# Gated cross-attention on one core: half of the next batch's context tiles turned a step earlier, and other instruction orders on all engines

## The reference

```python
q = (query @ wq)   # 32 heads of 128, rotated by position
k = (key @ wk)     # 8 groups of 128, each shared by 4 heads, rotated by position
v = (value @ wv)   # 8 groups of 128
raw = einsum('bhqd,bhkd->bhqk', q, k) / sqrt(128)
attn = softmax(raw + mask, axis=-1)
out = einsum('bhqk,bhkd->bhqd', attn, v) @ wo

x = x + tanh(g_xattn) * cross_attention(layernorm(x), ctx, ctx, mask)
x = x + tanh(g_ffn) * lora_experts(layernorm(x))
```

## Time and profile before

| | us |
|---|---|
| median of three runs (1941.01 to 1945.7) | 1941.62 |
| the profiled execution | 1944.6 |
| its span, first to last instruction | 1942.7 |

### The profile page before, as it was taken

The page is one execution under the profiler, slowest core; times in us unless marked ns, Lnnn a source line. Parts: engine busy times, 40 slices in busy tenths (PEclk is TensorE's granted clock), DMA queues, the critical chain, the costliest instruction groups (busy, mean ns, idle before and its releaser), DMA issues. The chain is left out here.

```text
span 1942.7 us, 36348 instructions
## 1 busy us (share of the span) xinstructions
PE 1863.1 (96%) x12454; PEld 1706.5 (88%) x12454; DVE 1552.9 (80%) x2598; ACT 1019.1 (52%) x1882; POOL 1194.0 (61%) x990
## 2 busy tenths in 40 slices
PE   7989999999999999999999999999999999999688
PEld 7979998999889998999899988999899988999576
DVE  6768888888878888888888888888788888888244
ACT  5645555555555555555655555555455555556232
POOL 5627666666666674777566666776576656777300
PEclk9999999999999999999999999999999999999788
DMA  6622111112111111221112211111121110211270
GB/s 221 251 73 37 36 21 32 26 37 31 31 32 34 32 16 33 37 36 21 31 26 36 31 23 30 32 35 20 31 32 31 30 33 13 56 16 21 60 249 20
DMA packets 75303, 91.98 MB, mean 47 GB/s; under 512 B 22948, under 2 KB 49828, under 8 KB 75144
## 3 DMA queue, kind: packets, MB, share of 16 engines
q1 hardware_dynamic: 74136, 83.44, 20.2%
q10 hardware_dynamic: 1008, 6.42, 0.8%
HBM read 74.07 MB, written 15.77 MB: 46 GB/s over the span
## 5 line engine op out<-in xcount | busy, mean ns | idle before, releaser
L699 POOL TENSOR_TENSOR pT<-prob,pT 125x448 fp32r<-125x448 f32 x384 | 483.8, 1271 | 86.1 <-ACT pT L824 86.1
L881 PE MATMUL low_banks<-wv_hi,cT_hi 128*125 128x256 f32 x1536 | 434.4, 283 | 0.0
L881 PE MATMUL low_banks<-wv_hi,cT_lo 128*125 128x256 f32 x1536 | 432.7, 282 | 0.0
L881 PE MATMUL low_banks<-wv_lo,cT_hi 128*125 128x256 f32 x1536 | 432.3, 281 | 0.0
L765 ACT ACTIVATE k_work<-low_banks 64x500 f32<-64x500 f32 x384 | 223.8, 583 | 193.3 <-PE low_banks L865 186.1
L1081 DVE TENSOR_TENSOR prob<-t_banks,mask_t 125x448 f32<-125x448 f32 x384 | 235.3, 618 | 110.2 <-PE t_banks L916 95.4
L693 POOL TENSOR_TENSOR k_lo<-k_work,k_hi 128x500 fp32r<-128x500 f32 x192 | 253.8, 1322 | 110.1 <-ACT k_hi L773 110.1
L865 PE MATMUL low_banks<-cT_hi,wk_hi 128*128 128x500 f32 x768 | 315.5, 411 | 0.4 <-DVE cT_lo L1052 0.4
L710 POOL TENSOR_TENSOR sums<-sums,prob 125x448 f32<-125x448 f32 x252 | 291.0, 1155 | 26.8 <-ACT prob L818 25.8
L865 PE MATMUL low_banks<-cT_lo,wk_hi 128*128 128x500 f32 x768 | 298.8, 389 | 0.0
L865 PE MATMUL low_banks<-cT_hi,wk_lo 128*128 128x500 f32 x768 | 298.5, 389 | 0.0
(11 more groups left out here) (152 smaller groups left out, 3857.0 us busy)
## 6 DMA issues: line engine op xcount, KB each, us to landing
stage<-in_ctx_dram SPq DMA_DIRECT2D x72, 250.0 KB
inv_b<-inv_by_head SPq DMA_DIRECT2D x65, 112.0 KB, 4.8
attn_by_head<-attn SPq DMA_DIRECT2D x65, 112.0 KB, 1.7
wq_raw<-in_L_xattn_wq_dram SPq DMA_DIRECT2D x7, 1024.0 KB, 6.8
q_raw<-q_by_head SPq DMA_DIRECT2D x64, 112.0 KB, 4.9
head_rows<-in_ctx_dram SPq DMA_DIRECT2D x24, 250.0 KB
stage<-in_L_xattn_wo_dram SPq DMA_DIRECT2D x4, 1024.0 KB, 6.9
k_work<-in_L_xattn_wo_dram SPq DMA_DIRECT2D x4, 1024.0 KB, 7.7
```

Source lines behind the costliest of these rows:

```text
L699: nc.gpsimd.tensor_tensor(pT[:, j % PT_SLOTS, :, 1, :], pair(j), f32(pT[:, j % PT_SLOTS, :, 0, :]), ALU.subtract).then_inc(p_lo, 1)
L881: mm = nc.tensor.matmul(v_banks[0:ST, m % 2, t * PAIR:(t + 1) * PAIR], cT[a][:, d, tile * ST:(tile + 1) * ST], w[1][mv][:, d, g * DH:g * D ...
```

## The change

Six of the twelve context tiles (C0 to C5) are turned in the step before the turn, which gets a row "ahead" of its own; C6 to C11 stay in the turn, where the mask turnings W0 and W1 move from the front to the middle. ScalarE copies the first pair of masked scores into the running maximum's bank ("copy", begin_top), so that DVE's first maximum reads it there rather than from SBUF. The rows of all kinds of step are written in another order. In the last step the projection of the first two groups goes by pass over all heads (O0h, O1h, O2h, then R0, R1, R2 for the second group), so that the high by high pass waits for no low part; later groups are projected by pass too. The first quarter of POOL's low part of wo moves into the step before, ahead of its last work. The third and fourth groups' loads are issued within the last batch's last step, the third's ahead of store_attn; the last inverse's round trip and the third group's low parts move behind the barrier.

```diff
-    "turn": ("W0 W1 C0 X C1 M C2 C3 V00 Y C4 K00 C5 K01 C6 K02 K03 C7 C8 PV0 V01 K10 K11 K12 C9 K13 V10 C10 C11 "
-           "V11 PV1 S0 S1 K20 K21 K22 K23 S2 PV2 S3 V20 V21 PV3 PV4 S4 S5 PV5"),
...
+    "ahead": ("K00 K01 K02 K03 V30 K10 K11 X C0 C1 M K12 K13 K20 K21 V31 Y PV0 K22 C2 C3 V40 S0 K23 V41 S1 V50 PV1 "
+            "PV2 S2 S3 V51 C4 C5 PV3 PV4 PV5 S4 S5"),
+    "turn": ("K00 K01 C6 C7 V00 K02 C8 X K03 M C9 Y V01 K10 K11 K12 C10 C11 K13 V10 PV0 W0 W1 K20 K21 K22 K23 V11 "
+           "PV1 PV2 V20 S0 S1 V21 S2 S3 PV3 S4 PV4 S5 PV5"),
...
-    "last": "X O00 M O01 Y O02 O03 PV0 PV1 PV2 PV3 PV4 PV5 Y1 O1",
...
+    "last": "O00 O01 O02 X O03 M O10 O11 Y O12 O13 O20 O21 O22 O23 R0 PV0 PV1 PV2 R1 R2 PV3 PV4 PV5 Y1",
...
+def context_item(b, m):
+
+    g = HKV - 2 if ("C", m) in t_fills(PE_STEP, "ahead") else HKV - 1
+    return t_item(b, g, "C", m, False)
...
-def output_loads(sp, shared, wo, attn_dram, i, passed):
-    for u in range(2):
-
-        sp.wait_ge(shared.attn_lo, i * 2 + (u + 1))
-        wait_apart(sp, shared.wo_lo, i * 2 + (u + 1), passed)
-        load_wo(sp, shared, wo, i * 2 + (2 + u), u)
-        load_attn(sp, shared, attn_dram, i * 2 + (2 + u), u)
+def output_load(sp, shared, wo, attn_dram, n, passed):
+
+    sp.wait_ge(shared.attn_lo, n - 1)
+    wait_apart(sp, shared.wo_lo, n - 1, passed)
+    load_wo(sp, shared, wo, n, n % 2)
+    load_attn(sp, shared, attn_dram, n, n % 2)
 
...
-                        wait_apart(sp, t_ready, t_item(b, g, "C", m - STAGE_RING, False) + 1, sp_passed)
+                        wait_apart(sp, t_ready, context_item(b, m - STAGE_RING) + 1, sp_passed)
                         load_context(nc, sp, shared, ctx_v, b + 1, m)
...
-                store_attn(b, g)
+                if g == HKV - 1 and last:
+                    output_load(sp, shared, wo, attn_dram, 2, sp_passed)
+                store_attn(sp, shared, attn_dram, b, g)
...
-        spread_inverse(B, 0)
-        output_loads(sp, shared, wo, attn_dram, 0, sp_passed)
-        store_attn(B, 0)
+        output_load(sp, shared, wo, attn_dram, 3, sp_passed)
...
-                    for h in range(REP):
-                        wo_low_head(h)
+                    wo_low_head(n)
...
+        def begin_top(n, item):
+
+            act.wait_ge(t_free, item + (RING + 1))
+            if n > 0:
+
+                act.wait_ge(subbed, n * PT)
+            nc.scalar.activation(run_max, pair(0), ACT.Copy).then_inc(top_begun, 1)
...
+                if what == "copy":
+                    begin_top(b * HKV + g + 1, t_item(b, g, "S", 0, last))
...
+                if what in ("O", "R"):
+                    u, part = ("O", "R").index(what), n[0]
+                    if what == "O" and n == (0, 0):
 
                         pe.wait_ge(k_rotated, k_item(b, g, NC - 1) + 1)
                         pe.wait_ge(v_free, v_item(b, g - 1, V_AHEAD - 1) + (RING + 1))
-                        pe.wait_ge(shared.wo_lo, 1)
-                    if h < REP - 1:
-                        pe.wait_ge(pieces, REP - 1 + h + 1)
-                    else:
-                        pe.wait_ge(shared.attn_lo, 1)
-                    mm = project_head(nc, shared, h, 0, True)
-                    if h == REP - 1:
+                    if part == 0:
+                        pe.wait_ge(shared.wo_hi, u + 1)
+                        pe.wait_ge(shared.attn_hi, u + 1)
+                    if part == 1:
+                        pe.wait_ge(*((pieces, n[1] + 1) if what == "O" and n[1] < REP - 1 else (shared.wo_lo, u + 1)))
+                    if part == 2:
+                        pe.wait_ge(*((pieces, REP - 1 + n[1] + 1) if what == "O" and n[1] < REP - 1 else (shared.attn_lo, u + 1)))
+                    heads = n[1:] if what == "O" else range(REP)
+                    for h in heads:
+                        mm = project_part(nc, shared, part, h, u, u == 0 and part == 0 and h == 0)
+                    if part == len(PASSES) - 1 and h == REP - 1:
                         mm.then_inc(shared.group_done, 1)
-                if what == "O" and n[0] == 1:
-                    project_group(nc, pe, shared, 1, 1)
...
-            if j > 1:
+            if j == 1:
+                dve.wait_ge(top_begun, n + 1)
+            else:
                 dve.wait_ge(topped, n * (PT - 1) + j - 1)
-            nc.vector.tensor_tensor(run_max, pair(0) if j == 1 else run_max, pair(j), ALU.max).then_inc(topped, 1)
+            nc.vector.tensor_tensor(run_max, run_max, pair(j), ALU.max).then_inc(topped, 1)
...
-                    dve.wait_ge(o_lo_copied, n_step + 1)
-                    dve.wait_ge(attn_ready, n_step + 1)
+                    made = n_step + n - (1 if kind == "last" else 0)
+                    dve.wait_ge(o_lo_copied, made + 1)
+                    dve.wait_ge(attn_ready, made + 1)
...
+def project_part(nc, shared, part, h, u, first):
+
+    a, m = PASSES[part]
+    for c in range(DC):
+        mm = nc.tensor.matmul(shared.low_banks[:, c, 0:TOK], shared.wo_s[a][:, u, h, c * P:(c + 1) * P],
+                              shared.attn_s[m][:, u, h].rearrange("p b s -> p (b s)"), start=first, stop=False,
+                              skip_group_check=True)
+    return mm
...
-def project_group(nc, pe, shared, g, u, first=False):
-    pe.wait_ge(shared.attn_lo, g + 1)
-    pe.wait_ge(shared.wo_lo, g + 1)
-    for h in range(REP):
-        mm = project_head(nc, shared, h, u, first)
+def project_group(nc, pe, shared, g, u):
+    pe.wait_ge(shared.wo_hi, g + 1)
+    pe.wait_ge(shared.attn_hi, g + 1)
+    for part in range(len(PASSES)):
+        if part == 1:
+            pe.wait_ge(shared.wo_lo, g + 1)
+        if part == 2:
+            pe.wait_ge(shared.attn_lo, g + 1)
+        for h in range(REP):
+            mm = project_part(nc, shared, part, h, u, False)
     mm.then_inc(shared.group_done, 1)
...
+        spread_inverse(nc, sp, shared, inv_dram, B, 0)
+        for n in (4, 5):
+            output_load(sp, shared, wo, attn_dram, n, sp_passed)
+        store_attn(sp, shared, attn_dram, B, 0)
...
-        with sp.Fori(1, pairs - 1) as i:
-            output_loads(sp, shared, wo, attn_dram, i, sp_passed)
+        for u in range(2):
+            sp.wait_ge(shared.attn_stored[u], 16 * (B * (HKV // 2) + 1 + u))
+        for n in (6, 7):
+            output_load(sp, shared, wo, attn_dram, n, sp_passed)
...
+        split_low(nc, dve, shared, 2, 0)
         split_low(nc, dve, shared, 3, 1)
+        normalise(nc, dve, shared, B, 0)
```

More of the change, by code:

```diff
@@ L100 @@
 POOL_STEP = {
[3 rows of a table removed]
[6 rows of a table added]
     "first": "klow0 klow1 klow2",
[2 rows of a table removed]
 }
 def step_kind(g, last):
-    return ("last" if last else "turn") if g == HKV - 1 else ("odd" if g % 2 else "even")
-def act_kind(g, last):
-    return "pre" if last and g == HKV - 2 else step_kind(g, last)
+    ends = ("pre", "last") if last else ("ahead", "turn")
+    return ends[g - HKV + 2] if g >= HKV - 2 else ("odd" if g % 2 else "even")
 def tasks(order):
@@ L157, in t_item @@
 def t_item(b, g, what, n, last):
-    kind = step_kind(g, last)
-    return b * BATCH_FILLS + (FIRST_FILLS + g * STEP_FILLS + t_place(kind, what, n))
+    before = sum(len(t_fills(PE_STEP, step_kind(e, last))) for e in range(g))
+    return b * BATCH_FILLS + (FIRST_FILLS + before + t_place(step_kind(g, last), what, n))
+def context_item(b, m):
+    g = HKV - 2 if ("C", m) in t_fills(PE_STEP, "ahead") else HKV - 1
+    return t_item(b, g, "C", m, False)
 def s_item(b, g, j):
@@ L731, in step @@
         def step(b, g, last):
-            for what, (n, *_) in tasks(POOL_STEP[act_kind(g, last)]):
+            for what, (n, *_) in tasks(POOL_STEP[step_kind(g, last)]):
                 if what == "klow":
@@ L812, in step @@
             done = b * (HKV * PT) + g * PT
-            for what, (n, *_) in tasks(ACT_STEP[act_kind(g, last)]):
+            for what, (n, *_) in tasks(ACT_STEP[step_kind(g, last)]):
                 s = ((g + 1) * NC + n) % 2
@@ L842, in step @@
                     v_high(v_item(b, g, n % V_AHEAD), n, done + n + 1 if g % 2 else max(done - PT + n + 1, 0))
+                if what == "copy":
+                    begin_top(b * HKV + g + 1, t_item(b, g, "S", 0, last))
                 if what == "chi":
-                    place = t_item(b, g, "C", n, last)
+                    place = context_item(b, n)
                     c_high(place, place % RING, n)
@@ L1254, in project, with output_part @@
     return mm
[L1257 to L1267 removed]
+def project_group(nc, pe, shared, g, u):
[8 more added lines that the diff above has]
+            mm = project_part(nc, shared, part, h, u, False)
     mm.then_inc(shared.group_done, 1)
[L1271 removed]
+def output_part(nc, ctx, shared, x, wo, a_in, b_in, wr, g_xattn, g_ffn, inv_dram, attn_dram, out):
     def sb(name, shape, dt=F32):
@@ L1542, in flamingo_block @@
         with ExitStack() as ctx:
[L1543 removed]
```

(1 more changed line is left out.)

86 lines of the change are left out of this document (40 added, 46 removed), and 64 rows, old and new, of tables (ACT_STEP, DVE_STEP, PE_STEP, POOL_STEP).

## The result

The changed kernel takes 1878.78 us (median of four runs, 1878.62 to 1880.07), the kernel before 1942.34 beside it on the same chip: a ratio of 0.9671, 95% interval 0.9659 to 0.9684. The profiled execution took 1878.95 us, 65.65 less than the 1944.6 of before.

The account below looks back on a forecast made before the run. TensorE bounds the kernel, with waits to gain in seven turns and at the last step and barrier. From 1944.6, -35.7 - 4.0 + 4.2 + 3.0 - 29.6 = -62.1 gave 1882.5 us; own range 1877 to 1888, outer 1866 to 1901.

Parts of the forecast that it names:

- both places: Where the prediction saw time to gain: the seven turns, and the last step with what follows.
- The turn and its floor: Step ahead 27.7 plus turn 28.4 us, 56.1 where 61.2 stood: 5.1 us in each of seven batches, 35.7 us.
- Tile 9: In the turn, a new wait for tile 9's load, issued behind norm and store: 0.6 us each, 4.2 for seven.
- Late loads: In one or two turns, a load coming late is no longer hidden: 3 us added, between 0 and 8.
- Late tiles: Rival: each of seven turns waits some 3 us more at C9 to C11, 21 us, 1903.5; chance 0.10.
- The long turns: Two turns 2 us longer at a low clock lose that: 4.0 us off the profiled execution, 1 off the median.
- ScalarE's copy: DVE's first maximum falls from 1443 to about 632 ns, ScalarE gets a 0.57 us copy; nothing on the path.
- Step before last: POOL's first quarter of wo's low part ahead of the third klow: a loss of 0 to 1.2 us, taken as 1.2.
- The last step: Last step and barrier: M at 1801.3, third group's loads at 1812.3, TensorE going on at about 1825.1; 29.6 us gained.
- From that point to the end nothing changes: Behind the barrier: 88 us of TensorE with its cover of loads stay as they were.
- slower: Rival: in 48 ordinary steps klow comes late for S4; at 1.6 us a step 1957; chance 0.04.
- no new waits: Rival: tiles 9 to 11 land on time in the turns, 7.2 us less, 1875; chance 0.18.

Follow-up runs that it names:

- loads_early: Changed kernel with the loads of tiles 9 to 11 sent a step earlier, from behind the query load: 1872.74 us, ratio 0.9624.
- norm_early: Changed kernel with DVE's norm ahead of the third maximum and last two masks in the step ahead of the turn: 1872.08 us, ratio 0.9629.
- nine_last: Changed kernel with the three loads at the turn's head sent in the order 10, 11, 9: 1922.39 us, ratio 0.9878.
- dve_begins: Changed kernel without ScalarE's copy, DVE forming the first maximum from two tiles in every step: 1879.43 us, ratio 0.9649.
- pre_free: Changed kernel; in the step before last, ScalarE's wo split goes behind the key work, POOL's first quarter behind the probability sums: 1879.32 us, ratio 0.9643.
- third_after_trip: Changed kernel with the third group's loads back behind both inverse round trips, ScalarE copying the last low half ahead of its splits: 1898.92 us, ratio 0.9803.
- heads_first: Changed kernel with the first group's projection by head again in the last step, X ahead of it: 1883.76 us, ratio 0.9669.

## Why the prediction held, step by step

1878.8 stands against 1882.5 and the range of its own, 1877 to 1888; both places were the right ones.

- *The turn and its floor.* Step ahead and turn were to take 27.7 + 28.4 = 56.1 us without waits; without the wait at tile 9 they take 55.9 and 56.0 (loads_early, norm_early). Right to 0.2 us. (The rows cut the turn off where S4 of the step ahead begins, 1.3 us before the turn's first key matmul; so they show 26.3 and 29.7 us in norm_early where the prediction has 27.7 and 28.4.) One reading was off: of the 5.1 us that the text calls waiting, show 36.10 - 32.44 = 3.7 as idle. The rest was longer busy time around the waits, 25.10 + 32.44 = 57.5 us in the old pair against 56.0 without waits, and it went with them.
- *Tile 9.* The place, the cause and the chain (norm behind the masks, store, loads) were right; two experiments that touch only this chain removed the wait. Its size was right too: 398.00 - 393.63 = 4.4 us of idle time in the seven pairs where 4.2 stood, 0.6 us each. It cost more than its idle time: the pairs are 56.9 - 56.0 = 0.9 us longer with it than without. That the three loads queue, at a DMA share of 0.31 after, is confirmed by nine_last. By the rule of the Trainium skill, DMA: Bandwidth & Descriptors, section Why a DMA increments its semaphore by 16 and not by 1, five engines of 16 carry them, and the trace agrees: 0.31 is 5 of 16.
- *Late loads.* The 3.0 us never came: no pair of the seven took over 57.1, and no wait at tile 9 was over 0.8. Late tiles did not come either: C10 and C11 never wait.
- *The long turns* went: the clock is 1.00 in all seven pairs. In all, the pairs gave 34.0 us where -35.7 - 4.0 + 4.2 + 3.0 = -32.5 stood.
- *ScalarE's copy*: 623 ns at the median, nothing on the path, with the copy or without it (dve_begins).
- *Step before last*: 26.9 us, 1.8 more than 25.1, where 1.2 stood as the upper bound. The text priced POOL's quarter at the third klow (0.49 us of idle time); the longer wait, 0.85 us, is at the second. That the second is late behind ScalarE's split, which the text named and did not price, fits pre_free, where both are moved and the step takes 25.1 us, but was not tested apart. pre_free did not make the end earlier.
- *The last step.* M was to come 4.6 us into the step (1801.3 - 1796.7) and came at 1767.53 - 1762.90 = 4.6; TensorE was to go on 28.4 us in and did at 29.0. From the start of the step before last this gave 28.4 us where 29.6 stood. third_after_trip shows that about 20 us of the gain at the end are the third group's loads, heads_first that about 4 are the early maximum, the low clock that each of these runs brings back included.
- *"From that point to the end nothing changes"*: wrong by 2.5 us, the one term put at nothing that was not nothing. The kernel before idled for 11 us there and started at the low level (0.50 in the first 5.35 us, which is 1.2 GHz); its 192 matmuls took 42.23 us. After a wait of 1.80 us the changed kernel starts at the full clock: 1791.89 to 1831.84 for the same 192, 39.95 us. The fifth group's loads, which were to have 15 us of cover, had 12.1 (1800.03 to 1812.12) and showed 0.53 us.
- *The sums.* Two don't come out. The lower end of the outer range, 1866, is about 1871 from the cases that it names (1882.5 - 7.2 - 1.2 - 3.0), and the 1957 of "slower" is 1959 (48 x 1.6 = 77). The forecast rests on neither. In it the pairs gave 1.5 us more than their terms and the last step 1.2 us less; that these two nearly cancel is luck.

Of the rivals, no new waits is what loads_early and norm_early made of it, at 1872 to 1873 where 1875 stood; TensorE waited for klow only in the step before last, never in the other steps.

## What to carry to other kernels

Count the instructions between two points of a schedule and price each from the trace: here that gave a floor that held to 0.2 us. Where the queue of one engine orders loads behind a result that they don't need, move either; but an engine without gaps, as POOL at the end here, handed the wait on to what it owed next. And price a wait on TensorE at more than its idle time: what comes behind it may run at half the clock, here up to 2.4 us more for 16 matmuls.
